# Attention with learned routing, first stage: one reciprocal for all heads, a reordered tail, and the next layer norm inside the turn

## What is computed

```python
xn = _layernorm(x)                          # (x - m) / sqrt(var + 1e-5)
s = _L0_attn_ref(xn, Wq, Wk, Wv, Wo)        # 16 heads, causal, weights (q.k / 4)^2
g = _silu(_L0_ffn_ref(xn, ...))
x = x + s * g
```

```python
A = (q @ k.T / 4) ** 2 * causal_mask        # 512 x 512, per head
o = (A @ v) / (A.sum(-1) + 1e-5)[:, None]   # then o of all heads @ Wo
```

```python
mlp = silu(xn @ Wg + bg) * (xn @ Wu + bu) @ Wd + bd
# routing: top 8 of 64 x-scores and of 64 y-scores for each of 4 heads, all
# 64 sums, top 8 of these, softmax over them; the weights of 512 experts
w = silu(xn @ down_embed[idx]) * softmax(scores)
out = mlp + w @ up_embed[idx]
```

## Time and profile before

| | us |
|---|---|
| median of 3 runs | 6478.83 (6478.44 to 6481.75) |
| profiled execution | 6476.3 |
| its span | 6474.1 |
| first stage, to the last addition to x | 1197.31 + 0.69 = 1198.0 |
| DVE busy in the whole span | 4304.2 (66%) |
| PE busy in the whole span | 5529.6 (85%) |

### The profile page before, as it was taken

How to read it: one execution, slowest core, us unless ns; L and a number is a source line. 1 busy time by engine, 2 the same in 40 slices (tenths; PEclk the granted TensorE clock), 3 DMA queues, 4 the chain that set the end, 5 groups by cost and what they waited for, 6 DMA issues and landing times. The chain is left out here.

```text
span 6474.1 us, 104407 instructions
## 1 busy us (share of the span) xinstructions
PE 5529.6 (85%) x31008; PEld 3052.4 (47%) x31008; DVE 4304.2 (66%) x6942; ACT 3742.1 (58%) x11798; POOL 2598.5 (40%) x2011
## 2 busy tenths in 40 slices
PE   6777777677777999899998999899998999999997
PEld 2333333222224555555555555555555555555554
DVE  6667666433335777777777777777777677777775
ACT  3344344223224776667676667666776677667775
POOL 1111222000003555455554555455555555555553
PEclk8888888777778999999999999999999999999998
DMA  0000000000002221222222222221222222222222
GB/s 37 0 0 0 0 0 0 20 0 0 0 0 82 47 50 47 53 54 48 49 52 51 51 49 48 53 54 47 48 49 56 51 47 49 56 51 50 47 49 66
DMA packets 160227, 244.42 MB, mean 38 GB/s; under 512 B 51280, under 2 KB 51280, under 8 KB 158928
## 3 DMA queue, kind: packets, MB, share of 16 engines
q1 hardware_dynamic: 159696, 238.08, 15.0%
HBM read 30.26 MB, written 6.29 MB: 6 GB/s over the span
## 5 line engine op out<-in xcount | busy, mean ns | idle before, releaser
L323 POOL TENSOR_TENSOR c_Pb<-c_Pb,c_rs 96x512 f32<-96x512 f32 (+1 forms) x960 | 996.7, 1038 | 1460.4 <-DVE c_rs L715 1460.4
L385 ACT ACTIVATE c_Pb<-c_S,c_nb 96x128 f32<-96x128 f32 (+1 forms) x3840 | 1344.2, 358 | 159.7 <-DVE c_nb L706 158.7
L722 DVE COPY c_PTs<-c_S 128x384 f32<-128x384 f32 (+1 forms) x960 | 558.2, 581 | 627.0 <-PE c_S L506 626.2
L706 DVE TENSOR_REDUCE c_nb<-c_S 96x4 f32<-96x512 f32 (+1 forms) x960 | 657.4, 685 | 403.2 <-PE c_S L496 402.9
L335 POOL TENSOR_TENSOR c_rot<-c_tAB 128x1024 f32<-128x1024 f32 x384 | 911.9, 2375 | 0.8 <-DVE c_tAB L685 0.8
L396 ACT ACTIVATE c_OT<-c_PO 128x192 f32<-128x192 f32 (+1 forms) x960 | 323.6, 337 | 772.9 <-PE c_PO L520 772.0
L385 ACT ACTIVATION_READ_ACCUMULATOR c_Pb<-c_S,c_nb 96x1 f32 (+1 forms) x3840 | 756.5, 197 | 0.0
L329 POOL TENSOR_TENSOR c_sqs<-c_sq 128x512 f32<-128x512 f32 x384 | 487.8, 1270 | 612.6 <-ACT c_sq L363 612.6
L496 PE MATMUL c_S<-c_QK 64*96 64x128 f32 (+1 forms) x7680 | 667.9, 293 | 0.0
L506 PEld LDWEIGHTS c_S<-c,c_Pb 96*128 96x128 f32 (+1 forms) x3840 | 434.8, 142 | 370.2 <-issue 215.6
L520 PE MATMUL c_PO<-c_PTs,c_V 128*64 128x96 f32 (+1 forms) x7680 | 557.6, 267 | 20.2 <-issue 19.2
(11 more groups left out here) (264 smaller groups left out, 10945.7 us busy)
## 6 DMA issues: line engine op xcount, KB each, us to landing
c_QK<-c_F SPq DMA_DIRECT2D x3072, 64.0 KB, 2.0
c_stage<-in_w_heads SPq DMA_DIRECT2D x36, 256.0 KB, 2.9
c_WT<-in_w_tails SPq DMA_DIRECT2D x6, 537.5 KB, 4.9
b_W<-in_w_level SPq DMA_DIRECT2D x1, 3133.0 KB, 10.3
a_W<-in_w_level SPq DMA_DIRECT2D x1, 3078.0 KB, 10.3
c_WT<-in_w_tails SPq DMA_DIRECT2D x6, 512.0 KB, 3.7
x<-in_x SPq DMA_DIRECT2D x1, 2048.0 KB, 7.4
x_kept<-x SPq DMA_DIRECT2D x1, 2048.0 KB, 6.3
```

Of the source, the lines that this page charges most:

```text
L323: nc.gpsimd.tensor_tensor(p, p, r, ALU.mult).then_inc(*p_ready.up())
L385: e = nc.scalar.activation(Pb[0:m, n % 3, i, :], S[0:m, 2 * (n % 2) + r, c * SPAN_K:(c + 1) * SPAN_K], ACT.Exp, bias=nb[0:m, n % 2, i:i + ...
L706: nc.vector.tensor_reduce(nb[0:m, n % 2].rearrange("p (b c) -> p b c", b=2), S[0:m, b:b + 2, 0:2 * SPAN_K].rearrange("p b (c k) -> p b c k ...
L722: nc.vector.tensor_copy(PTs[:, n % 2].rearrange("p (b c) q -> p b c q", b=2)[:, :, :, 0:m], S[:, b:b + 2, 2 * SPAN_K:].rearrange("p b (c q ...
```

## The change

It does five things in `level0`.

- The column of ones of head group g now lies in value column 8 + g, so each group of four heads has its denominators in its own row of the 32. The selection matrix takes all four: PE accumulates four matmuls over `U` into one bank (`gathered`), DVE takes one reciprocal of it, and four new matrices (`A_SPR`, 512 columns) spread the reciprocals to each group's rows. DVE's `divide(g)` is then one multiplication that reads PSUM.
- The tail stands ahead of the fourth routing tile on DVE; ACT's `routing(3)` comes behind the copies of the first three transposed tiles.
- The mean, centring, squares, variance and root of the next sequence are issued inside the current turn, and its `xn` inside `route(3)`. The first sequence's are ahead of the loop, and the last turn is written out behind it, without them.
- The products of `hT` come ahead of the transposes, in bank 6; s is in bank 7, transposes in banks 4 and 5. PE waits for `out_done` ahead of the first head's values instead of ahead of the mean.
- `hT` shares its buffer with `gs`; the last multiplication writes `rden`.

```diff
-A_EPS = A_SEL + P
-A_LOWQ = A_EPS + 1
+A_SPR = A_SEL + P
+A_EPS = A_SPR + 4 * P
+A_LOWQ = A_EPS + 4
...
-ROUTED = (1, 6, 11, 15)
+ROUTED = (1, 6, 11)
...
-        hT = sb("hT", [P, 4, SEQ])
+        hT = gs
...
-                pool.wait_ge(*ones_set.nth(1))
-                nc.gpsimd.memset(V[:, :, :, 8:9], 1.0).then_inc(*ones_set.up())
+                for g in range(4):
+                    pool.wait_ge(*ones_set.nth(g + 1))
+                    nc.gpsimd.memset(V[:, :, 4 * g:4 * g + 4, 8 + g:9 + g], 1.0).then_inc(*ones_set.up())
...
+                def squares(turn):
+                    act.wait_ge(*centred.nth(1, turn))
+                    nc.scalar.activation(csq[:, :], cen[:, :], ACT.Square).then_inc(*squared.up())
+                def root(turn):
+                    act.wait_ge(*var_done.nth(1, turn))
+                    nc.scalar.activation(csq[:, :], B[:, 1, :], ACT.Ln, bias=col["eps5"]).then_inc(*lnv.up())
+                    act.wait_ge(*lnv.nth(1, turn))
+                    nc.scalar.activation(rstd[:, :], csq[:, :], ACT.Exp, scale=-0.5).then_inc(*rstd_ready.up())
+                def body(turn, following):
...
+                    nc.scalar.preload_act_table_set("natural_log_exp_and_others")
+                    if following is not None:
+                        squares(following)
+                    def turned(t):
                         act.wait_ge(*mt_done.nth(t + 1, turn))
                         nc.scalar.activation(MT[:, :, t * TILE:(t + 1) * TILE],
-                                                         B[:, 6 + t % 2, :].rearrange("p (b t) -> p b t", b=4), ACT.Copy).then_inc(*mt_ready.up())
+                                             B[:, 4 + t % 2, :].rearrange("p (b t) -> p b t", b=4), ACT.Copy).then_inc(*mt_ready.up())
+                    if following is not None:
+                        root(following)
+                    for t in range(TILES - 1):
+                        turned(t)
+                    routing(TILES - 1, turn)
+                    turned(TILES - 1)
                     act.wait_ge(*ffn_done.nth(1, turn))
-                    nc.scalar.activation(sgate[:, :], B[:, 2, :], ACT.Silu, bias=W[:, A_BD:A_BD + 1]).then_inc(*gate_ready.up())
-                    nc.scalar.preload_act_table_set("natural_log_exp_and_others")
+                    nc.scalar.activation(sgate[:, :], B[:, 6, :], ACT.Silu, bias=W[:, A_BD:A_BD + 1]).then_inc(*gate_ready.up())
                     for q in mine:
                         q.full()
+                squares(0)
+                root(0)
+                with act.Fori(0, seqs - 1) as turn:
+                    body(turn, turn + 1)
+                body(seqs - 1, None)
...
+                def mean(turn):
+                    nc.tensor.matmul(B[:, 0, :], ones_mean, x[:, bass.ds(turn * SEQ, SEQ)], start=True, stop=True).then_inc(*mean_done.up())
+                def variance(turn):
+                    pe.wait_ge(*squared.nth(1, turn))
+                    nc.tensor.matmul(B[:, 1, :], ones_mean, csq[:, :], start=True, stop=True).then_inc(*var_done.up())
+                def body(turn, following):
...
-                    pe.wait_ge(*out_done.nth(0, turn))
...
+                        if h == 0:
+                            pe.wait_ge(*out_done.nth(0, turn))
...
-                    def spread(g):
-                        pe.wait_ge(*u_ready.nth(4, turn))
-                        if g >= 2:
-                            pe.wait_ge(*rden_ready.nth(g - 1, turn))
-                        nc.tensor.matmul(B[:, 6 + g % 2, :], W[:, A_SEL:A_SEL + P], U[:, g, :], start=True, stop=True).then_inc(*den_done.up())
-                    spread(0)
-                    spread(1)
-                    for c in range(4):
+                    pe.wait_ge(*u_ready.nth(4, turn))
+                    for g in range(4):
+                        mm = nc.tensor.matmul(B[:, 6, :], W[:, A_SEL:A_SEL + P], U[:, g, :], start=g == 0, stop=g == 3)
+                    mm.then_inc(*gathered.up())
+                    def up(c):
                         if c >= 2:
                             pe.wait_ge(*h_ready.nth(c - 1, turn))
                         nc.tensor.matmul(B[:, 4 + c % 2, :], W[:, A_U + c * P:A_U + (c + 1) * P], xn[:, :], start=True, stop=True).then_inc(*up_done.up())
+                    def spread(g):
+                        pe.wait_ge(*rden_ready.nth(1, turn))
+                        if g >= 2:
+                            pe.wait_ge(*o_ready.nth(g - 1, turn))
+                        nc.tensor.matmul(B[:, 7 - g % 2, :], W[:, A_SPR + g * P:A_SPR + (g + 1) * P], rden[:, :], start=True, stop=True).then_inc(*den_done.up())
+                    up(0)
+                    up(1)
+                    spread(0)
+                    spread(1)
+                    up(2)
+                    up(3)
                     spread(2)
                     spread(3)
+                    pe.wait_ge(*gs_ready.nth(4, turn))
+                    if following is not None:
+                        mean(following)
                     pe.wait_ge(*o_ready.nth(4, turn))
-                    pe.wait_ge(*gs_ready.nth(4, turn))
                     for g in range(4):
-                        mm = nc.tensor.matmul(B[:, 1, :], W[:, A_O + g * P:A_O + (g + 1) * P], U[:, g, :], start=g == 0, stop=g == 3)
+                        mm = nc.tensor.matmul(B[:, 7, :], W[:, A_O + g * P:A_O + (g + 1) * P], U[:, g, :], start=g == 0, stop=g == 3)
                     mm.then_inc(*s_done.up())
+                    if following is not None:
+                        variance(following)
+                    pe.wait_ge(*h_ready.nth(4, turn))
+                    for c in range(4):
+                        nc.tensor.matmul(B[:, 6, :], W[:, A_D + c * P:A_D + (c + 1) * P], hT[:, c, :], start=c == 0, stop=False, skip_group_check=True)
                     for t in range(TILES):
                         pe.wait_ge(*m_ready.nth(t + 1, turn))
                         if t >= 2:
                             pe.wait_ge(*mt_ready.nth(t - 1, turn))
                         for b in range(4):
-                            mm = nc.tensor.transpose(B[:, 6 + t % 2, b * P:(b + 1) * P], M[:, t, b * P:(b + 1) * P], ident)
+                            mm = nc.tensor.transpose(B[:, 4 + t % 2, b * P:(b + 1) * P], M[:, t, b * P:(b + 1) * P], ident)
                         mm.then_inc(*mt_done.up())
-                    pe.wait_ge(*h_ready.nth(4, turn))
-                    for c in range(4):
-                        nc.tensor.matmul(B[:, 2, :], W[:, A_D + c * P:A_D + (c + 1) * P], hT[:, c, :], start=c == 0, stop=False)
                     pe.wait_ge(*mt_ready.nth(4, turn))
                     for b in range(4):
-                        mm = nc.tensor.matmul(B[:, 2, :], W[:, A_UP + b * P:A_UP + (b + 1) * P], MT[:, b, :], start=False, stop=b == 3)
+                        mm = nc.tensor.matmul(B[:, 6, :], W[:, A_UP + b * P:A_UP + (b + 1) * P], MT[:, b, :], start=False, stop=b == 3, skip_group_check=True)
                     mm.then_inc(*ffn_done.up())
                     for q in mine:
                         q.full()
+                mean(0)
+                variance(0)
+                with pe.Fori(0, seqs - 1) as turn:
+                    body(turn, turn + 1)
+                body(seqs - 1, None)
...
+                def centre(turn):
+                    dve.wait_ge(*mean_done.nth(1, turn))
+                    nc.vector.tensor_tensor(cen[:, :], x[:, bass.ds(turn * SEQ, SEQ)], B[:, 0, :], ALU.subtract).then_inc(*centred.up())
+                def normal(turn):
+                    dve.wait_ge(*rstd_ready.nth(1, turn))
+                    nc.vector.tensor_tensor(xn[:, :], cen[:, :], rstd[:, :], ALU.mult).then_inc(*xn_ready.up())
+                def route(t, turn, following=None):
...
+                    if following is not None:
+                        normal(following)
...
-                    for t in range(TILES):
+                    for t in range(TILES - 1):
                         route(t, turn)
                     def divide(g):
                         dve.wait_ge(*den_done.nth(g + 1, turn))
-                        if g:
-                            dve.wait_ge(*o_ready.nth(g, turn))
-                        nc.vector.reciprocal(rden[:, :], B[:, 6 + g % 2, :]).then_inc(*rden_ready.up())
-                        dve.wait_ge(*rden_ready.nth(g + 1, turn))
-                        nc.vector.tensor_tensor(U[:, g, :], U[:, g, :], rden[:, :], ALU.mult).then_inc(*o_ready.up())
-                    divide(0)
-                    divide(1)
-                    for c in range(4):
+                        nc.vector.tensor_tensor(U[:, g, :], U[:, g, :], B[:, 7 - g % 2, :], ALU.mult).then_inc(*o_ready.up())
+                    def gate(c):
                         dve.wait_ge(*up_done.nth(c + 1, turn))
                         dve.wait_ge(*gs_ready.nth(c + 1, turn))
```

(38 more changed lines are left out.)

24 lines of the change are left out of this document (5 added, 19 removed).

## The result

The changed kernel takes 6386.36 us (median of 4 runs, 6374.81 to 6387.49) where the kernel before takes 6478.64: a ratio of 0.9853, interval 0.9836 to 0.987. Measured a second time (changed_again) it took 6376.69 against 6478.65, ratio 0.984 (0.9824 to 0.9856). The forecast was 6398, range 6368 to 6452.

The account below looks back on a forecast made before the run. DVE works almost without pause through four routing tiles, then a serial chain follows. Seven turn starts save 81.2 us; 2.4 more, 3 less and 0.9 more give 80.9 less: 6398 us, range 6368 to 6452.

Parts of the forecast that it names:

- Start of the next turn: From the addition's end to the next memset: 20.9 us instead of 32.5, 11.6 saved in each of seven turns.
- The gather's wait: DVE idle ahead of the only reciprocal until PE's gather matmuls end: a new wait of 12.4 us per turn.
- The wait in the fourth tile: DVE waits about 4 us for ACT's small exponentials, behind the copies, where there was no wait.
- The wait for the Silu: DVE's idle time ahead of the last multiplication: about 7.5 us against 15.94.
- The low stretches: PE clock at 1.2 GHz after short gaps: about 1.6 us added to the tail, 1.5 ahead of the s matmuls.
- the tail: DVE from the reciprocal through gates, divisions and centring: 13.3 us, was 22.0, ending 83.5 after the memset.
- The finish: Last tile's transposes, MT matmuls, Silu, multiplication and addition: 9.1 us, ending at R + 114.6; before 17.3.
- R + 63.5: R is the turn's memset on DVE; heads ending at another point than 63.5 us after it would refute the prediction.
- the rival with the fast clock: PE keeps its clock in the two short gaps: tail 11.8, fourth tile 20.5, 103 us less, 6375; chance 0.25.
- The fourth tile beside POOL: Without POOL masks beside it, the fourth tile loses about another microsecond at its front; the sum stays, exponentials hold it.
- Once per run: Larger weights W, 257.5 KB more on 3078.0 KB that took 10.3 us, at the start: +0.9 us.

Follow-up runs that it names:

- no_inner_norm: Changed kernel with the layer norm of a sequence back at the start of its own turn; median 6453.9 us, ratio 0.996 to the kernel before.
- exp_first: Changed kernel with ACT's fourth-tile exponentials ahead of its copies of the first three transposed tiles; median 6352.9 us, ratio 0.9807.
- warm: Changed kernel with eleven extra PE matmuls between the third and the last tile's transposes; median 6366.9 us, ratio 0.9834.
- one_recip: Changed kernel with fourth tile ahead of the tail, norm in its own turn, PE's finish in old order; single reciprocal kept; 6376.4 us, ratio 0.9845.
- tile_back: Changed kernel with the fourth routing tile and its exponentials back ahead of the tail, one reciprocal and inner norm kept; 6329.3 us, ratio 0.9773.
- packed: As tile_back, with PE's finish work moved under earlier waits and two gates ahead of the reciprocal; 6237.22 us, ratio 0.9621.
- warm_full: As warm, with twelve extra matmuls and one more ahead of the MT matmuls; median 6364.2 us (of three), ratio 0.982.

## Why the prediction was right, and where it was not

*Start of the next turn.* Foretold 20.9 from the addition to the memset, measured 20.7 in every turn. no_inner_norm shows that it is the norm inside the turn. The prediction split the gain into 7.2 of norm and the projections' low clock. The low clock is about 2: from the first projection to the memset it was 25.2 (765.05 to 790.22) and is 23.2. The remaining 2.5 are the projections running ahead of the addition.

*The new waits.* The gather's wait was to be 12.4 and is 11.99. The wait in the fourth tile, released by ACT, was to be about 4 and is 3.95; exp_first shows that it comes from ACT's order alone. The wait for the Silu was to be about 7.5 and is 8.47, by the low stretch below.

*The low stretches.* This is the step that was mis-sized, three times. One was laid on the tail, behind a gap taken as 1.9 us: the gap is 1.73 and in the 14 turns of two profiles that have a next one no stretch follows, so the tail is 11.7 and not 13.3. One was laid on the s matmuls: the gap of 2.09 is there, and a stretch follows in 3 of 14 turns, where the tile takes 22.2 to 22.3; the others have 20.6 and not 22.0. The finish was given 9.1 and has 10.0 in this turn, since the stretch behind the idle 10.73 covers more of the MT matmuls (5.79, foretold 4.6). The heads are a smaller term: the prediction names their end at another point than R + 63.5 as a sign of being wrong, and they end at 62.4 to 62.7 here and at 62.4 to 64.1 in changed_again. That is worth about 0.5 us of this turn, beyond the 0.5 that the sum had. Together the addition comes at 111.9 to 113.2 and not at 114.6.

Over eight turns the stretch from memset to addition is 15.7 us shorter than before, where the forecast's sum has 0.6 (8 x 0.3 lost, 3 gained in the last turn). This is most of the distance between the 81 us foretold and the 99.4 by which the first stage ends earlier; the start of the turns and the first memset give 1.7 and 1.8.

So the trace is that of the rival with the fast clock, which had a chance of 0.25: tail 11.7 where it has 11.8, tile 20.6 where it has 20.5, no stretch in most turns. By the end of the first stage, 99.4 and 97.1 less, its 103 is nearer than the forecast's 81. Of the medians one (6386.4) lies halfway between 6398 and 6375 and the other (6376.7) at the rival's. That the forecast's time is within 0.2% of the first is thus partly luck: the path is right, and the stretches that it added aren't there in most turns. The rival's sum takes 1.6 for the last turn instead of 3, without a row; the last turn's addition is at 109.1 and 109.5, about 3 earlier than the others.

The from which the stretch was taken were of another place, among the heads, and a gap's length alone doesn't tell whether a stretch comes: warm has the same gaps with and without one.

The page that spoke for this rival, the Trainium skill's TensorE: Matmul & The Clock Gate, Part 1 (ramp penalty under 1% of a typical span), is neither borne out nor refuted for the whole span: the finish alone costs 2.5 us a turn, 20 of 6375 or 0.3%, and the other low stretches, of a run whose mean granted clock is 0.931, are not in that count. These 20 us are a fifth of what the change gave, so for an edit of this size they count.

*The fourth tile beside POOL.* From its first instruction to the end of the large sum it took 6.6 before (701.59 to 708.23) and takes 5.7 now (671.53 to 677.24), with no masks beside it. It agrees with the rule of the Trainium skill's SBUF — State Buffer, "Who interferes with whom", which the prediction used: the tile is 0.9 us shorter. As foretold it gives nothing, since DVE then waits for ACT.

*A sentence that was wrong.* The prediction said that the reciprocals saved "and the tail moved ahead bring nothing by themselves", and treated the two as one step of 0.3 us. one_recip shows 105.8 us for the reciprocals with their order, no_inner_norm 81.0 lost by the tail's new place, and the norm then gives back 72 to 75. Even the two together, no_inner_norm, end the first stage 24.8 earlier than before. The three differences add up to the change's 99 by the way they are taken, one after another; in another order they are others, as tile_back shows. The waits that ate the gain were named and priced; that they belong to one part, which could be left out, was not seen before the parts were run apart.

*Once per run.* The first memset comes at 57.9 in one profile and 59.3 in the other, 58.8 before: the 0.9 for the larger weights can't be told from that.

## What to carry to other kernels

Price each part of a composite change by itself, against the order without it: a sum near zero can hide a part that gains as much as the whole and one that takes it back. And price it with the other parts in place too, since the tail's place cost 81 us without the norm inside and 42 to 44 with it. Moving work ahead of other work on the busiest engine pays only if its inputs are there; here the tail waited 12 us for PE while the routing tile that could have filled the time stood behind it. And when the last stretch of a loop is serial, put whatever doesn't depend on the last result under earlier waits, until one engine works through without a gap: from tile_back to packed this took 88.8 us off the first stage, nearly as much as the whole change, and packed as a whole 230.0.

## What the runs showed of the hardware

In warm, TensorE's clock fell to the lower level behind gaps of 1.29 and 0.69 us after 9.6 us of dense matmuls, in six turns of eight, and stayed high behind the same gaps in two; in tile_back it stayed high behind a gap of 0.69 in eight of eight. Behind a gap of 1.73 between the up products and the spreads it fell in none of the 50 turns that had it (of seven profiles), behind one of 2.09 ahead of the s matmuls in 3 of 14 turns of the changed kernel and in six of seven of tile_back, and behind 4.47 to 4.77 in all 14 turns that had it (one_recip and tile_back). With no gap over about half a microsecond, in warm_full and packed, it was 1.00 in the stretch looked at. A RECIPROCAL of 128x512 float32 from PSUM took 3.36 us on VectorE, a multiplication of the same size 0.69. Untouched stages of 5275 us differed by up to 18 us between profiled executions.
